# The first feed-forward begun inside the attention tail in front of it, and the next attention's projections begun inside its own tail

## The reference

```python
x = layernorm(x + attn0(x))      # 32 heads of 16, 8 key heads, causal; output projection w_dense, bias

# feed-forward 0, on h = x
query = h @ Wq.T                                    # 64 wide
rk    = aux_keys @ Wr.T                             # 128 slots, 48 wide
router_scores = (query @ Wr.T) @ rk.T / sqrt(48) + log_rel
top_idx = top_k(router_scores, 8)
attn = query @ aux_keys[top_idx].T / sqrt(64) + log_rel[top_idx]
w    = softmax(attn)                                # over the 8 chosen slots
aux_out = (w @ aux_values[top_idx]) @ Wvd.T @ Wvu.T
var  = log1p(var(h));   norm_var = var / (mean(var) + 1e-6)
learned = gelu(h @ Wu1.T + bu1) @ Wu2.T + bu2
u    = clip(0.5 * norm_var + 2.5 * sigmoid(learned), 0, 5)
gate = sigmoid(w1 * clip((u - 0.5) / 1.5, 0, 1) + bias);  gate = 0 where gate < 0.05
x = layernorm(x + h + gate * aux_out)

x = layernorm(x + attn1(x))      # 32 heads of 128, 8 key heads, rotary embedding
```

## Time and profile before

| | |
|---|---|
| median of three executions | 2038.09 us (2034.04 to 2041.58) |
| profiled execution, its own time | 2040.56 us |
| span of the profile | 2038.6 us, 29630 instructions |
| TensorE busy | 1911.4 us (94%) |
| VectorE, ScalarE, GpSimd busy | 1144.3, 843.4, 845.6 us (56%, 41%, 41%) |
| mean granted clock of TensorE | 0.976 |

### The profile page before, as it was taken

How to read it: one execution, slowest core, us unless ns; L and a number is a source line. 1 busy time by engine, 2 the same in 40 slices (tenths; PEclk the granted TensorE clock), 3 DMA queues, 4 the chain that set the end, 5 groups by cost and what they waited for, 6 DMA issues and landing times.

```text
span 2038.6 us, 29630 instructions
## 1 busy us (share of the span) xinstructions
PE 1911.4 (94%) x10936; PEld 1276.9 (63%) x10936; DVE 1144.3 (56%) x2195; ACT 843.4 (41%) x1855; POOL 845.6 (41%) x1363
## 2 busy tenths in 40 slices
PE   6999967999999999999999799999999898999897
PEld 3545435888888888888887687864444454544343
DVE  5666456666666666666667324136556355566345
ACT  1565423444444444444445333323555403565420
POOL 2554316545454545454544444323444312343301
PEclk9999978999999999999999899999999999999999
DMA  6112000101010101010100234112222102111101
GB/s 215 36 42 99 1 11 1 53 1 52 1 52 1 53 1 53 1 52 1 52 1 32 80 107 173 50 28 68 64 61 93 32 1 80 33 42 47 46 0 42
DMA packets 46209, 94.59 MB, mean 46 GB/s; under 512 B 7689, under 2 KB 35721, under 8 KB 43145
## 3 DMA queue, kind: packets, MB, share of 16 engines
q1 hardware_dynamic: 43474, 90.34, 13.4%
q10 hardware_dynamic: 2592, 2.36, 0.5%
HBM read 61.68 MB, written 2.10 MB: 31 GB/s over the span
## 4 chain that ended last, share of the span: by engine, by line
PE 79%; DVE 11%; ACT 4%; issue 3%; DMA 1%; POOL 1%; POOLq 0%; SPq 0%; ACTq 0%; DVEq 0%
PE PS L1368 9%; PE PS L1449 9%; PE PS L452 6%; PE PS L555 6%; PE PS L1868 5%; PE PS L533 5%; PE PS L499 5%; PE PS L580 4%; PE PS L1427 4%; PE PS L1881 3%; PE PS L1379 3%; PE PS L1411 3%; PE PS L1839 2%; PE PS L467 2%; DVE NM L744 2%
## 5 line engine op out<-in xcount | busy, mean ns | idle before, releaser
L965 ACT ACTIVATE PB<-PS 128x512 f32<-128x512 f32 x480 | 280.9, 599 | 236.0 <-PE PS L533 233.0
L872 POOL TENSOR_SCALAR_AFFINE_SELECT PB<-PB 128x256 f32<-128x256 f32 (+1 forms) x480 | 174.2, 367 | 318.1 <-ACT PB L965 312.0
L744 DVE TENSOR_REDUCE NM<-PS 128x2 f32<-128x1024 f32 x192 | 209.2, 1091 | 168.0 <-PE PS L501 166.5
L499 PE MATMUL PS<-KQ 96*128 96x512 bf16 (+3 forms) x768 | 185.4, 306 | 17.4 <-DVE NM L744 11.0
L533 PE MATMUL PS<-KQ 99*128 99x512 bf16 (+3 forms) x768 | 182.6, 303 | 4.9 <-ACT PB L965 3.6
L1766 POOL TENSOR_SCALAR PR<-PR,RCP 128x512 f32<-128x512 f32 (+3 forms) x256 | 135.4, 539 | 106.7 <-DVE RCP L1564 106.5
L1577 DVE TENSOR_REDUCE NX<-PS 128x1 f32<-128x512 f32 (+3 forms) x256 | 124.8, 488 | 77.5 <-PE PS L1400 71.9
L452 PE MATMUL PS<-XTT,WA 128*128 128x512 f32 x288 | 145.2, 610 | 13.6 <-DVE ident_masks_b L2406 12.1
L1635 ACT CAST OTH<-PS 128x512 fp32r<-128x512 f32 x64 | 37.6, 587 | 281.9 <-PE PS L1432 281.9
L501 PE MATMUL PS<-ident_masks_b 128*128 128x128 bf16 x768 | 149.1, 223 | 0.0
L280 POOL TENSOR_TENSOR rstd<-ve,halfneg 128x1 f32<-128x1 f32 x64 | 44.8, 700 | 250.6 <-DVE ve L257 250.6
(11 more groups left out here) (306 smaller groups left out, 4558.1 us busy)
## 6 DMA issues: line engine op xcount, KB each, us to landing
KQ<-HI SPq DMA_DIRECT2D x90, 128.0 KB, 2.4
KQ<-MID SPq DMA_DIRECT2D x72, 128.0 KB, 2.4
WB<-f_w SPq DMA_DIRECT2D x12, 768.0 KB, 4.4
WB<-w1o SPq DMA_DIRECT2D x8, 1024.0 KB, 8.0
WC<-f_w SPq DMA_DIRECT2D x10, 768.0 KB, 4.4
WB<-w1a SPq DMA_DIRECT2D x8, 768.0 KB, 4.4
WB<-w1b SPq DMA_DIRECT2D x8, 768.0 KB, 5.9
WA<-w SPq DMA_DIRECT2D x6, 1024.0 KB, 6.3
```

The costliest lines, as they stand in the source:

```text
L499: pe.matmul(ps, KQ[0:SR, self.query(G, h), i * P:(i + 1) * P], KQ[0:SR, self.key(G, h), 0:n], start=True, stop=False)
L744: x = dve.tensor_reduce(nm[:, h:h + 2, i], PS[:, b:b + 2, 0:(i + 1) * P], AX.X, ALU.max, negate=True)
L872: pool.affine_select(blocks, blocks, [[0, count], [1, P]], ALU.is_ge, 0.0, base=0, channel_multiplier=-1).then_inc(s16["probs_ready"].sem, 1)
L965: act.activation(PB[:, n % PBS, :], PS[:, 4 + n % 2, :], ACT.Exp, scale=self.scale)\
```

## The change

There are three parts.

- **Inside the tail of `a0`.** The tail's loops are written out with two hooks, `follow` and `follow_scalar`, which do nothing for the third and fourth attention. For the first (`First16`) they call `Ffn0.begin` and `Ffn0.begin_scalar`: TensorE makes `rk`, `av`, the query of batch 0, `g` and `p` between the tail's y tiles and transposes, in banks 6 and 7, and ScalarE instead of VectorE copies them.
- **Choices ahead of the gate.** In `Ffn0.tensor` the router scores of both batches come first, with the query of batch 1 between them, and then both u products. ScalarE copies the second query, and makes the high parts of the weights before the gelus instead of between the exponentials. GpSimd makes both low parts here (`B1L` was made in `a1`).
- **The next attention begun in the tail.** In the tail of `Ffn0`, y stays in banks 4 and 5 for both batches, and TensorE makes the values (`project_v`) at step 6, the high parts of two projections (`begin_high`, 8 products each) at steps 8 and 9, and their low parts (`begin_low`, 4 each) behind the last transposes. `a1.tensor` begins with the third projection. GpSimd's `x_low` pieces lie one behind each root from tile 1 on. In `a1` the first two `rope_low` run on VectorE.

```diff
@@ Attention16.tensor / scalar
-                self.tails[1].tensor(pe)
+                tail = self.tails[1]
+                for t in range(NT + 2):
+                    if t < NT:
+                        self.y_tile(pe, t, PS[:, t, :]).then_inc(tail.s_y.sem, 1)
+                    self.follow(pe, t)
+                    if t >= 2:
+                        if t >= 4:
+                            pe.wait_ge(tail.s_t.sem, tail.s_t.at(t - 3))
+                        tail.turn(pe, t - 2, PS[:, tail.t_bank(t - 2), :])
-                self.tails[1].scalar(act)
+                for t in range(NT):
+                    self.follow_scalar(act, t)
+                    self.tails[1].take(act, t, PS[:, self.tails[1].t_bank(t), :])
@@ Ffn0
+            def begin(self, pe, t):
+                if t == 1:
+                    pe.wait_ge(S_f0.sem, 16)
+                    self.products(pe, PS[0:48, 6, 0:P], [(f0_WrT, f0_keysT)], "rk_psum")
+                    self.products(pe, PS[0:32, 7, 0:P], [(f0_Wvd[:, c, :], f0_avT[:, c, :]) for c in range(NC)], "av_psum")
+                elif t == 2:
+                    pe.wait_ge(f0["rk_ready"].sem, 1)
+                    self.query(pe, 0)
+                elif t == 3:
+                    pe.wait_ge(f0["av_ready"].sem, 1)
+                    self.products(pe, PS[0:64, 7, 0:P], [(f0_Wr, RKT[:, :])], "g_psum")
+                elif t == 4:
+                    pe.wait_ge(f0["q_ready"].sem, 1)
+                    self.products(pe, PS[:, 6, :], [(AVT[:, :], f0_WvuT)], "p_psum")
+            def begin_scalar(self, act, t):
+                if t == 0:
+                    act.wait_ge(f0["rk_psum"].sem, 1)
+                    act.copy(RKT[:, :], PS[0:48, 6, 0:P]).then_inc(f0["rk_ready"].sem, 1)
+                    act.wait_ge(f0["av_psum"].sem, 1)
+                    act.copy(AVT[:, :], PS[0:32, 7, 0:P]).then_inc(f0["av_ready"].sem, 1)
+                    act.mul(G[:, P:2 * P], f0_keysT, 0.125).then_inc(f0["g_ready"].sem, 1)
+                    act.wait_ge(f0["q_psum"].sem, 1)
+                    act.copy(QF[:, 0, :], PS[0:64, 6, :]).then_inc(f0["q_ready"].sem, 1)
+                elif t == 1:
+                    act.wait_ge(f0["g_psum"].sem, 1)
+                    act.mul(G[:, 0:P], PS[0:64, 7, 0:P], 1.0 / np.sqrt(48.0)).then_inc(f0["g_ready"].sem, 1)
+                elif t == 2:
+                    act.wait_ge(f0["p_psum"].sem, 1)
+                    act.copy(PT0[:, :], PS[:, 6, :]).then_inc(f0["p_ready"].sem, 1)
@@ Ffn0.tensor
-                pe.wait_ge(S_f0.sem, 16)
-                ...
+                pe.wait_ge(f0["g_ready"].sem, 2)
+                self.route(pe, 0)
+                self.query(pe, 1)
+                self.route(pe, 1)
+                pe.wait_ge(f0["p_ready"].sem, 1)
                 for b in range(NB):
-                    ...
+                    mms(PS[:, 6 + b, :], [(f0_Wu1[:, c, :], XTT[:, b, c, :]) for c in range(NC)], "u_psum")
+                pe.wait_ge(f0["gelu_ready"].sem, NB)
                 ...
-                        if t >= 2:
-                            pe.wait_ge(self.tails[b].s_v.sem, self.tails[b].s_v.at(t - 1))
+                        if n >= 2:
+                            before, u = self.tails[(n - 2) // NT], (n - 2) % NT
+                            pe.wait_ge(before.s_v.sem, before.s_v.at(u + 1))
                         self.y_tile(pe, b, t).then_inc(self.tails[b].s_y.sem, 1)
                     ...
+                    if n == 6:
+                        pe.wait_ge(self.tails[0].s_t.sem, self.tails[0].s_t.at(NT))
+                        a1.project_v(pe, 0)
+                    if n in (8, 9):
+                        a1.begin_high(pe, n - 8)
                     ...
+                for p in (0, 1):
+                    a1.begin_low(pe, p)
@@ Ffn0.scalar
+                act.wait_ge(f0["q_psum"].sem, 2)
+                act.copy(QF[:, 1, :], PS[0:64, 7, :]).then_inc(f0["q_ready"].sem, 1)
+                a1.high(act, 0, "a")
+                a1.high(act, 0, "b")
                 ...
-                    if b == 0:
-                        a1.high(act, 0, "a")
-                        a1.high(act, 0, "b")
@@ Ffn0.gpsimd
                 a1.low(pool, 0, "a")
+                a1.low(pool, 0, "b")
                 self.tails[0].gpsimd(pool)
                 for t in range(NT):
                     self.tails[1].root(pool, t)
-                    if t == 2:
-                        a1.x_low(pool, 0, (0,))
-                a1.x_low(pool, 0, (1, 2, 3))
+                    if t >= 1:
+                        a1.x_low(pool, 0, (t - 1,))
+                a1.x_low(pool, 0, (3,))
@@ Attention1
+            def begin_high(self, pe, p):
+                pe.wait_ge(s1["a_hi"].sem, 1)
+                pe.wait_ge(s1["a_lo"].sem, 1)
+                pe.wait_ge(s1_xh.sem, NC)
+                for i, w in enumerate((A1H, A1L)):
+                    for c in range(NC):
+                        pe.matmul(PS[:, p, :], w[:, c, (P, 0)[p]:(P, 0)[p] + P], XH[0][:, c, :],
+                                  start=(c == 0 and i == 0), stop=False)
+            def begin_low(self, pe, p):
+                for c in range(NC):
+                    pe.wait_ge(s1_xl.sem, c + 1)
+                    x = pe.matmul(PS[:, p, :], A1H[:, c, (P, 0)[p]:(P, 0)[p] + P], XL[0][:, c, :],
+                                  start=False, stop=(c == NC - 1))
+                x.then_inc(s1["proj"].sem, 1)
@@ Attention1.tensor / vector / gpsimd
-                for p in (0, 1):
-                    for _ in self.project(pe, p):
-                        pass
-                self.project_v(pe, 0)
                 ...
                 self.rope(dve, 1)
+                self.rope_low(dve, 0)
                 self.take_v(dve, 0)
+                self.rope_low(dve, 1)
                 self.rope(dve, 2)
                 ...
-                self.low(pool, 0, "b")
                 for p in range(3):
                     self.sum(pool, p)
-                    self.rope_low(pool, p)
+                self.rope_low(pool, 2)
```

71 lines of the change are left out of this document (28 added, 43 removed).

## The result

| | before | after |
|---|---|---|
| median (6 runs each) | 2038.76 us | 2028.59 us |
| lowest to highest | 2034.04 to 2041.58 | 2024.25 to 2030.58 |
| profiled execution, its span | 2040.56, 2038.6 | 2030.24, 2028.5 |
| mean granted clock of it | 0.976 | 0.977 |

What follows compares the result with a forecast made beforehand. TensorE held 79% of the chain and VectorE 11%, yet gaps were left in the stages touched. -0.9 + 12.0 - 2.4 + 6.7 = 15.4 us saved, 0.75% of the 2038.09 median, gives 2022.7; range 2016.5 to 2030.

Steps and rivals of the forecast that it cites:

- four stages: Last tiles of first attention to first scores of second, cut at two barriers and the weights' turning; 87.80 us before.
- signs that I gave for being wrong: Masks after the first exponential's end; clock 0.5 in the head's first 5 us or the projections; ScalarE waiting for VectorE.
- Head of the feed-forward: From the first barrier to the turned weights: 24.0 us instead of 35.95, 12.0 shorter; bounds 9.5 to 13.
- rival 1: Clock falls between last p product and barrier, so routes and query run at half: some 2.4 us, 2025.1; chance 0.17.
- Holds beside GpSimd: In the feed-forward's head, VectorE's choices held twice by GpSimd's low parts, up to 3 us; masks at 15 to 18.
- Rival 2: VectorE stays the head's bound: larger holds, second mask at 20 to 21, not 18; 3 us, 2025.7; chance 0.07.
- Tail of the first attention: Up to the first barrier: y3 1.4 us late, 0.5 back from transposes; 0.9 longer, 12.45; bounds 0.5 to 2.
- Tail of the feed-forward: From turned weights to second barrier: VectorE waits 1.9 us for y7; 2.4 longer, 28.5; bounds 1 to 5.
- Start of the second attention: From second barrier to first scores: 7.5 us instead of 14.2, 6.7 shorter; bounds 5.5 to 7.3.
- Rival 3: Inserted values and projections delay VectorE over 1.9 us; last two stages' 4.3 gain halves or goes, 2025 to 2027; chance 0.08.
- rival 4: TensorE, spread thin by insertions, stays at half clock throughout: 28 us lost against 15.4, 2050.8; chance 0.03.
- stretch behind the scores: From the second attention's first scores to its fourth rope: unchanged, as rope 2 starts together with the scores as before.

Runs made afterwards that it cites:

- filled_tail: The changed kernel with three unread products added in TensorE's gaps at the end of the first attention's tail; 2026.17 us, ratio 0.9930 to the kernel before.
- after_again: The changed kernel run once more, unaltered, for a second look at where its clock falls; 2026.45 us, ratio 0.9931 to the kernel before.
- undo_choices: The changed kernel with u product, query and router scores batch by batch again, mask and exponential in turn; 2033.54 us, ratio 0.9969 to the kernel before.
- y3_first: The changed kernel with all four y tiles ahead of the feed-forward's products in the attention's tail, p copied later; 2023.54 us, ratio 0.9911 to the kernel before.
- value_pieces: The changed kernel with the value projection made tile by tile and the first projections' high parts moved; 2025.45 us, ratio 0.9913 to the kernel before.

## Why the prediction was right, and where it missed

**Direction and mechanism: right, the size short.** Each of the four stages moved the way that was forecast, by the mechanism forecast, and no new wait came that wasn't named. But 10.2 us came of 15.4, and the time is inside the range only because that takes in the rivals and 2 us for scatter: the forecast's own bounds ended at 2026. Of the 5.9 us that the point is too low the four stages hold 4.0, and 3.1 of these are one term. The head's gain of 8.8 is also below its own lower bound (9.5). Two of the signs that I gave for being wrong did appear: the clock of 0.5 in the first 5 us of the head, and one in the projections (0.50 from 321.3 to 324.7), which cost nothing on the path, as the third projection still ended 0.6 us ahead of the first scores.

**Head of the feed-forward, the term that was mis-sized.** Forecast 24.0 (-12.0), measured 27.12 (-8.8). The step that failed is the start of its count, "routes 1.95, query of batch 1 3.6, so 5.55" at the full clock. They took 3.50 and 5.41 to 5.47: 8.9, so 3.4 us more. With that in its place the sum of the prediction gives 27.4. It is rival 1, given 0.17 and priced at 2.4 us; both were too small. It had the argument for it in the earlier trace rows, a fall in a similar gap at 259.0, and I set against it the 3.6 us of query that now come before. filled_tail refutes that: with the same query and its gaps filled the clock stays at 1.00 and the head is 23.90. So what counted was the gap between the p products and the barrier (TensorE waits 0.52, 0.36 and 0.71 us there, with only two groups of transposes between) and not the work ahead of it. The price was short since I took from the earlier trace rows only the 4.8 us of half clock that lay behind the barrier then. The half clock lasts as long as it did, 6.8 us (263.3 to 270.1, before 259.2 to 266.0), but it begins 0.3 us behind the barrier instead of 2.0 ahead of it, so all of it lies in the head, and half of that is the 3.4. The moment of the fall moved by 1.1 us against the barrier over the seven executions. By the Trainium skill (TensorE: Matmul & The Clock Gate, Part 1) the moment of a change moves from run to run; that agrees with these, and with after against after_again. It did not help with whether the clock falls in the head of after, as there it fell in every execution.

**The rest of the head: right.** Second routes 1.99, u 7.08, gelu 0.69, load, exponentials 1.15, load: the terms of the sum to 0.1 us. Holds beside GpSimd: one of 1.24 us on the second choice (1.67 where the same line on the first choice took 0.43), where two with up to 3 us were allowed. The masks were ready 18.9 us behind the barrier where 15 to 18 were counted, since VectorE got the second scores only at 11.6, behind the slow routes and query; the first exponential started at 20.7. Rival 2 did not come, but undo_choices shows that it is no idle one: 3.1 us on the path where the order was the old one. The table loads: 1.28 each, and the next instruction starts 0.02 behind the load's end (283.65 behind 282.35 + 1.28). The 1.38 us of drain for each switch that the Trainium skill states (ScalarE: Activation LUTs, What ACT_TABLE_LOAD costs) are in none of them; by the page's figure the head would be some 1.4 longer than the 27.4 (an estimate), and it is 27.12.

**Tail of the first attention: right in kind, 0.6 off.** Forecast +0.9, measured +1.5: y3 was there 2.0 us late rather than 1.4. Counted from VectorE's start on tile 0, the query began 3.14 us in where 2.88 was counted, 0.26 of the 0.5; the rest is y3's own 1.02 for 0.9 and small gaps. The give-back of 0.5 by full-clock transposes came. y3_first shows that the cost is all y3's place.

**Tail of the feed-forward: right.** Forecast +2.4, measured +2.7, the wait for y7 2.06 (1.9). value_pieces takes 2.05 of it away. **Start of the second attention: right** to 0.04 us, which is in part luck: the terms that I named add up to 7.2 and not to 7.5, and the hold of VectorE beside GpSimd took 0.84 (1.53 for 0.69) where 0.5 was counted. **Rival 3** (fillers pushing VectorE further) and **rival 4** (half clock all through) did not come: the clock of the feed-forward's tail is 0.87, above the 0.83 of before.

**The whole against the stages.** The four stages give -11.33, the stretch behind the scores +0.55, together -10.8; the spans differ by 10.1. The other 0.7 lies spread over the rest of the program and I can't place it. The stretch behind the scores was forecast as unchanged, and the +0.55 is no effect of the change: the profiled executions of before and of after both lost clock there. The other two profiled executions of after, which kept it, took 8.84. That may be a part, and is not all, of the difference between the medians, 10.2 us there and 15.7 and 13.8 us in the two later sets. What else differs between those sets was not found.

## What to carry to other kernels

Follow work that you move into a gap to the next barrier, and price the products behind the barrier at both clocks. Here short idle times ahead of the barrier went with half clock behind it in seven executions of seven, and a few unread products, or the real ones in another order, were worth 3 us where the clock was kept. Put products in the tail of a stage in the pieces in which their inputs come ready and behind the tile that another engine waits for: the value projection as one block cost 2.05 us more than in pieces, and the y tile behind a query 1.5 more than in front of it. When masks or other VectorE work on SBUF run beside long GpSimd instructions, count a hold as long as what is left of GpSimd's instruction, and order the work so that something else covers it.

## What was not expected of the hardware

- The hold of VectorE by GpSimd has no fixed size: 1.53 us for 0.69 beside an addition of 1.01, 1.67 for 0.43 and 1.50 for 0.54 beside subtractions, and 3.79 for 0.69 beside one of 3.60. Each ended 0.2 to 0.6 us behind the end of a GpSimd instruction. The choice's maxima and replacements, on tiles of 128 columns, took 0.87 and 0.28 beside the same GpSimd instruction and in front of it, and the mean and variance of a tile of 512 columns (L255) took its usual 0.69 beside a GpSimd instruction that ran from 307.62 to 308.89: not every VectorE instruction is held.
- The same instruction stream keeps the clock in one execution and loses it in another (after: 0.52 or 1.00 behind the scores; y tiles first: 1.96 or 2.81 us for the same routes, with the same idle times ahead). In a kernel of 2 ms such a fall is worth 1.8 to 3.4 us, which is of the size of what was to be measured; the stages of a trace tell these apart, the medians don't.
